# Attention passages split in PSUM, maxima four to a step with the mask added on VectorE, and a first gate in three ranges beside the mixing layer

## What is computed

```
x = x + ln(rwkv_block(ln(x)))      # time mixing (a scan), then channel mixing: squared relu, 512 wide
x = x + ln(moe_16(ln(x)))          # 16 experts of 64, grouped top-4 gate, plus a shared one of 128
x = x + ln(delta_net(ln(x)))       # 16 heads of 8, two decaying memories, q, k with rotary positions
x = x + ln(gqa_moe(ln(x)))         # h = x + gqa(rms(x)); h + moe of 8 dense experts, top 2
```

```
gate:  scores = sigmoid(x @ w_gate.T); best 2 of 4 groups; best 4 experts of these; weights normed
gqa:   attn = q k^T / sqrt(8), causal: where(j <= i, attn, -inf); softmax; @ v    # 16 heads of 8, 4 kv heads
```

## Time and profile before

| | us |
|---|---|
| median of 3 runs | 1586.7 (1578.39 to 1589.89) |
| profiled execution | 1584.72 |
| its span | 1583.5 |
| PE, DVE, ACT, POOL busy | 1204.8, 1098.2, 715.5, 697.1 |
| granted TensorE clock, mean | 0.878 |

### The profile page before, as it was taken

The page is one execution under the profiler, slowest core; times in us unless marked ns, Lnnn a source line. Parts: engine busy times, 40 slices in busy tenths (PEclk is TensorE's granted clock), DMA queues, the critical chain, the costliest instruction groups (busy, mean ns, idle before and its releaser), DMA issues.

```text
span 1583.5 us, 19095 instructions
## 1 busy us (share of the span) xinstructions
PE 1204.8 (76%) x6080; PEld 571.9 (36%) x6080; DVE 1098.2 (69%) x2477; ACT 715.5 (45%) x1576; POOL 697.1 (44%) x849
## 2 busy tenths in 40 slices
PE   3414988999998567665649687998899889989873
PEld 1212454555554223232313232444343434343222
DVE  5888546455555699898959675868686878687032
ACT  4644682255555201212130266556565556555741
POOL 7324672455455387858550122133412441244244
PEclk9756987999999698787865698999999999999995
DMA  3000013222220000020225101111010201000010
GB/s 102 0 1 7 38 51 70 74 63 66 62 73 27 11 0 1 0 55 0 45 40 79 23 1 26 35 17 33 4 32 14 37 4 32 4 1 2 2 40 14
DMA packets 33634, 46.99 MB, mean 30 GB/s; under 512 B 4991, under 2 KB 18175, under 8 KB 33215
## 3 DMA queue, kind: packets, MB, share of 16 engines
q1 hardware_dynamic: 30942, 43.84, 12.9%
q10 hardware_dynamic: 2592, 1.93, 0.4%
HBM read 39.08 MB, written 6.68 MB: 29 GB/s over the span
## 4 chain that ended last, share of the span: by engine, by line
PE 38%; DVE 29%; POOL 14%; issue 10%; ACT 8%; DMA 1%; ACTq 0%; POOLq 0%; DVEq 0%
PE PS L585 9%; DVE SS L1074 6%; PE PS L540 5%; PE PS L568 5%; DVE RB L991 3%; DVE RB L992 3%; PE PS L630 3%; PE PS L377 2%; ACT RB L1448 2%; POOL RB L1616 2%; POOL rs L1515 2%; PE PS L255 2%; DVE st L675 2%; PE PS L363 2%; DVE PS L980 2%
## 5 line engine op out<-in xcount | busy, mean ns | idle before, releaser
L1448 ACT ACTIVATE RB<-PS 128x512 f32<-128x512 f32 (+3 forms) x768 | 326.2, 497 | 288.0 <-PE PS L568 286.7
L1074 DVE TENSOR_REDUCE SS<-PS 128x1 f32<-128x512 f32 (+3 forms) x768 | 374.2, 548 | 76.4 <-PE PS L543 64.6
L540 PE MATMUL PS<-B 96*128 96x512 bf16 (+3 forms) x768 | 258.0, 355 | 52.0 <-DVE B L1117 21.3
L1682 POOL TENSOR_SCALAR_AFFINE_SELECT RB<-RB 128x512 f32<-128x512 f32 x128 | 81.2, 634 | 429.6 <-ACT RB L1448 429.5
L568 PE MATMUL PS<-B 96*128 96x512 bf16 (+3 forms) x768 | 235.5, 334 | 29.8 <-ACT RB L1448 28.7
L585 PE MATMUL PS<-RB,B 128*32 128x512 f32 (+3 forms) x1536 | 169.5, 513 | 8.2 <-ACT RB L1455 7.9
L1616 POOL TENSOR_TENSOR RB<-RB,B 128x512 f32<-128x512 f32 x64 | 83.5, 1307 | 132.2 <-DVE RB L926 99.3
L540 PEld LDWEIGHTS PS<-B 96*128 96x128 bf16 x768 | 77.1, 101 | 160.0 <-DVE SS L1074 83.6
L445 PE MATMUL PS<-RB,w_hspread 128*128 128x512 f32 x128 | 80.6, 764 | 61.9 <-POOL RB L1638 52.3
L926 DVE TENSOR_TENSOR RB<-RB,PS 128x512 f32<-128x512 f32 x72 | 49.0, 682 | 110.1 <-ACT RB L1327 80.4
L543 PE MATMUL PS<-w_msk,w_identb 128*128 128x128 bf16 x512 | 118.8, 234 | 0.0
(11 more groups left out here) (229 smaller groups left out, 2044.0 us busy)
## 6 DMA issues: line engine op xcount, KB each, us to landing
B<-scrW SPq DMA_DIRECT2D x128, 128.0 KB, 3.0
B<-scrQ SPq DMA_DIRECT2D x72, 128.0 KB
scrQ<-B SPq DMA_DIRECT2D x6, 384.0 KB, 2.6
B<-scrK SPq DMA_DIRECT2D x36, 64.0 KB
X<-in_x SPq DMA_DIRECT2D x8, 256.0 KB, 9.7
out_dram<-X SPq DMA_DIRECT2D x8, 256.0 KB, 3.0
B<-in_w SPq DMA_DIRECT2D x3, 576.0 KB, 4.6
B<-in_zeros SPq DMA_DIRECT2D x9, 128.0 KB
```

Source lines behind the costliest of these rows:

```text
L540: ins = pe.matmul(p[:, 0:w], qs[u % 3][:, h, 128 * i:128 * i + 128], keys_of(u, h)[:, 512 * c:512 * c + w], start=True, stop=not diagonal)
L1074: dve.tensor_reduce(MX[:, u % 2, i, h, c:c + 1], bank(bank_of["first", u, n])[:, 0:first_width(i, c)], AX, ALU.max).then_inc(s["mx1"], 1)
L1448: act.activation(RB[:, 4 * (step % 3) + z, 0:w], bank(bank_of["score", step, z])[:, 0:w], ACT.Exp).then_inc(s["ex2"], 1)
```

## The change

Three edits.

1. The passages. The rest (L1046) is written back into its PSUM bank; the second part is a ScalarE copy out of PSUM; the third part is subtracted on VectorE out of PSUM. R2 is gone. The banks are given back after the third part. The two memsets of slice 6 go from VectorE to GpSimd.
2. The maxima. The mask matmul is gone. `highest` takes diagonal products with `tensor_tensor_reduce`: it adds the mask (128 x 512 bf16, zeros then the triangle), writes the sum back to PSUM and the maximum to MX. Unit 1's maxima stay five to a step; from step 20 on those of units 2 to 7 go four to a step without a gap.
3. The first gate. Three ranges of 8, 8 and 16 tiles instead of two halves. Units 0, 1, 2 of the experts stand in steps 20, 21, 22 of the mixing layer, the cuts of range 0 in unit 2. Range 1 is routed in the experts' steps 3 to 8, range 2 in 11 to 17. Banks, rows and the order of SP's loads follow.

```diff
+        def maxima_at(step):
+            if step < 20:
+                return [(1, n) for n in range(5 * step, min(5 * step + 5, 96))]
+            return [(2 + m // 96, m % 96) for m in range(4 * (step - 20), 4 * (step - 20) + 4) if m < 6 * 96]
...
+        RANGES = [(0, 8), (8, 8), (16, 16)]
+        FIRST_UNIT = 20
...
             def cut_n(g):
-                pe.wait_ge(s["cut_n"], g // 4 + 1)
-                i = 4 if g >= 4 else 0
+                pe.wait_ge(s["cut_n"], range_of(g) + 1)
+                i = 1 + g if g < 2 else next_d()
...
+            def experts(v):
+                if v == 2:
+                    cut_n(0)
+                    cut_n(1)
+                if 0 <= v - 3 < 9 * NG:
+                    out_m(v - 3)
+                if 9 <= v < 11:
+                    cut_n(v - 7)
+                if 18 <= v < 22:
+                    cut_n(v - 14)
+                for g, k in head_slices(v):
+                    head_d(g, k)
+                if v < 9 * NG:
+                    gate_up_m(v)
...
+                if step >= FIRST_UNIT:
+                    experts(step - FIRST_UNIT)
+            for v in range(NG + 15 - FIRST_UNIT, MOE_STEPS):
+                experts(v)
...
-                diagonal = c == i // 4
-                ins = pe.matmul(p[:, 0:w], qs[u % 3][:, h, 128 * i:128 * i + 128],
-                                keys_of(u, h)[:, 512 * c:512 * c + w], start=True, stop=not diagonal)
-                if diagonal:
-                    ins = pe.matmul(p[:, w - 128:w], identb[:, :], msk[:, 0, :], start=False, stop=True)
-                ins.then_inc(s["mm1"], 1)
+                pe.matmul(p[:, 0:w], qs[u % 3][:, h, 128 * i:128 * i + 128],
+                          keys_of(u, h)[:, 512 * c:512 * c + w], start=True, stop=True).then_inc(s["mm1"], 1)
...
             def highest(u, n):
-                dve.tensor_reduce(MX[:, u % 2, i, h, c:c + 1], bank(bank_of["first", u, n])[:, 0:first_width(i, c)],
-                                  AX, ALU.max).then_inc(s["mx1"], 1)
+                w = first_width(i, c)
+                p = bank(bank_of["first", u, n])[:, 0:w]
+                if c == i // 4:
+                    ins = dve.tensor_tensor_reduce(p, p, msk[:, 512 - w:512], 1.0, LOWEST, ALU.add, ALU.max,
+                                                   MX[:, u % 2, i, h, c:c + 1])
+                else:
+                    ins = dve.tensor_reduce(MX[:, u % 2, i, h, c:c + 1], p, AX, ALU.max)
+                ins.then_inc(s["mx1"], 1)
...
                 if k == 6:
                     stats(b, x_tile, "e", 8)
-                    own.done(dve.memset(batch(B[4], b), 0.0))
-                    own.wait()
-                    dve.memset(VA[:, 8 * b:8 * b + 8, :, 8:9].rearrange("p i k e -> p (i k) e"), 1.0).then_inc(s["va_e"], 1)
                 if k == 9:
-                    cut_e(b, 0, cutq[b][0], R2[b][:, 0:512], 128, 8.0 ** -0.5, s["cq_e"])
+                    rest_e(b, 0, cutq[b][0], 128, 8.0 ** -0.5)
                     if b:
                         dve.wait_ge(s["sk_e"], 32 * b)
-                    cut_e(b, 1, cutk, R2[b][0:64, 512:1024], 64, 1.0, s["ck_e"])
+                    rest_e(b, 1, cutk, 64, 1.0)
+                    last_e(b, 0, cutq[b][0], 128, s["cq_e"])
+                    last_e(b, 1, cutk, 64, s["ck_e"])
                 if k == 10:
-                    cut_e(b, 2, cutq[b][1], R2[b][:, 0:512], 128, 8.0 ** -0.5, s["cq_e"])
+                    rest_e(b, 2, cutq[b][1], 128, 8.0 ** -0.5)
+                    last_e(b, 2, cutq[b][1], 128, s["cq_e"])
...
-            def cut_e(b, n, o, rest, rows_, scale, last):
+            def rest_e(b, n, o, rows_, scale):
                 p = bank(bank_of["pj_e", b, n])[0:rows_, :]
                 dve.wait_ge(s["r_e"], 4 * b + n + 1)
-                dve.scalar_tensor_tensor(rest, p, scale, o[:, 0, :], ALU.mult, ALU.subtract).then_inc(s["cut_e"], 1)
-                dve.wait_ge(s["cut_e"], 3 * b + n + 1)
-                own.done(dve.tensor_copy(o[:, 1, :], rest))
-                own.wait()
-                dve.tensor_tensor(o[:, 2, :], rest, o[:, 1, :], ALU.subtract).then_inc(last, 1)
+                dve.scalar_tensor_tensor(p, p, scale, o[:, 0, :], ALU.mult, ALU.subtract).then_inc(s["cut_e"], 1)
+            def last_e(b, n, o, rows_, last):
+                p = bank(bank_of["pj_e", b, n])[0:rows_, :]
+                dve.wait_ge(s["cm_e"], 3 * b + n + 1)
+                dve.tensor_tensor(o[:, 2, :], p, o[:, 1, :], ALU.subtract).then_inc(last, 1)
...
+                    for n, o, rows_ in ((0, cutq[b][0], 128), (1, cutk, 64)):
+                        act.wait_ge(s["cut_e"], 3 * b + n + 1)
+                        act.activation(o[:, 1, :], bank(bank_of["pj_e", b, n])[0:rows_, :], ACT.Copy).then_inc(s["cm_e"], 1)
...
+            def experts(v):
+                if v == 3:
+                    score_n(2)
...
+                if step == 17:
+                    score_n(0)
+                if step == 19:
+                    score_n(1)
...
+            weights_out(0)
+            for m in range(4):
+                for h in range(2):
+                    sp.dma_start(CW[m][64 * h:64 * h + 64, :],
+                                 scrW[2 * m + h:2 * m + h + 1, 0:512].to_broadcast([64, 512])).then_inc(s_w[m], 16)
             sp.wait_ge(s["vv_b"], 8)
             sp.dma_start(WW[:, :, :], I["wL1"]).then_inc(s["w_ww"], 16)
             sp.dma_start(cs, I["rope"]).then_inc(s["w_cs"], 16)
...
-                if m == 24:
+                if m == 12:
                     weights_out(1)
+                if m == 26:
+                    weights_out(2)
```

230 lines of the change are left out of this document (123 added, 107 removed).

## The result

| | before | after |
|---|---|---|
| median | 1585.7 us (4 runs) | 1562.7 us (4 runs, 1558.6 to 1565.1) |
| profiled execution (span) | 1584.7 (1583.5) | 1561.3 (1560.0) |
| ratio | | 0.986, 95% interval 0.981 to 0.990 |

The change gave 23 us (1.4%) where 52 were predicted. The new time lies in the predicted range (1505 to 1575), which reaches that far only because it takes in the rivals (two of them at 1557 and 1559). The likeliest case did not happen: the direction came out, the size did not. Ratios are always against the kernel before as measured beside each kernel; its medians ran from 1584.7 to 1589.3 us, so medians of different experiments compare to a few us only. All medians here are of undisturbed executions; one of the four of the kernel with plain maxima took 4702 us and is left out. Where the time went is read first from the same views as before.

What follows compares the result with a forecast made beforehand. It took VectorE to bound the scan stage and TensorE, with VectorE close behind, the last attention. 1584.7 less 34 (attention), 14 (passages) and 4 (gate) gives 1532.7, so 1533 us, range 1505 to 1575.

Steps and rivals of the forecast that it cites:

- The likeliest case: Whole kernel: all three parts gain as forecast, giving 1533 us, own range 1505 to 1553, chance 0.60.
- Where VectorE's work counts in the scan stage: Layer 1's scan with the passages: VectorE bounds the stretch, so work taken off it gains 14 us, between 5 and 16.
- The stretched L1050: Passages: subtraction falls from 2.31 to 0.69 us with its source in PSUM, five times, 8.1 us gained; casts go, 4.9.
- The memsets: Passages, slice 6: moving the memset of 1024 elements from VectorE to GpSimd gains 2.7 us and delays only the passage.
- Slice 10's bank: Passages: TensorE's slice 10 waits for the last part instead of the rest, a step later, so costed at nothing.
- The attention: Last attention: 5.6 us per unit, 39 in seven units, less 5.1 in unit 0, so 34 us gained, between -9 and 67.
- the masks: Last attention: dropping 64 mask matmuls per unit frees TensorE, 3.2 us gained per unit, between 2.6 and 3.8.
- the spreading: Last attention: four maxima in every step from step 20, instead of five in most, gains 3.3 us per unit, between 0 and 6.
- the dearer maxima: Last attention: maxima that add the mask cost VectorE 0.08 us more each, giving back 0.9 us per unit.
- the prediction's third rival: Last attention: no gain on TensorE, masks lie in time it waits anyway, spreading only moves queues; 1557 us, chance 0.13.
- the two rivals of a dearer maximum: Last attention: new maximum 0.2 us dearer gives 1559 us, chance 0.12; at half rate, 0.33 dearer, 1616 us, chance 0.10.
- The gate: First gate: only eight tiles and two cuts come before the first experts, 4 us gained, between -3 and 8.

Runs made afterwards that it cites:

- the kernel with plain maxima: Changed kernel with plain maxima in place of the maxima that add the mask, causal mask left out of the computation: 1561.0 us, ratio 0.983.
- the order put right in both kernels: Slice 10 put behind the next batch's slice 1 and the value products, in the changed kernel (1557.7 us) and in the kernel before (1579.9 us).
- the other order alone: Kernel before with only slice 10 put behind the next batch's slice 1 and the value products: 1579.9 us, ratio 0.996.
- with nothing in their place: Kernel before with the mask matmuls left out, plain maxima still five to a step: 1576.1 us, ratio 0.993.
- the division first: VectorE's division ahead of its step's maxima: kernel before 1569.4 us, with only the mask in the maximum 1561.7, with only four maxima a step 1548.8, changed kernel 1541.9.
- the masks alone: Kernel before with the mask added by VectorE in the maximum, maxima still five to a step: 1579.2 us, ratio 0.995.

## Why the prediction was right or wrong

**Where VectorE's work counts in the scan stage** was the step that failed first: 14 us predicted, minus 1.4 measured. I read "VectorE busy 195 of 224 us" as "VectorE sets the end" for the whole stretch, so that each microsecond off it came out. In most steps it does set the end: in 5.6 of 5.6 us without a passage, in 13.2 of 13.4 with slice 9, and there the work that went came out nearly whole (3.9 and 3.5 us of work, 3.6 us of time each). But 87% is an average, and more than half of the work that went stood where VectorE stands still or then began to: the memsets in the steps of slices 6 and 7, where GpSimd's rstd and the addition behind it end last; slice 10, where the held bank and TensorE's queue then ended last (no idle time before, 4.4 and 4.6 us after); and the end, where VectorE had 17.5 idle of 31.4 us. VectorE did 17.1 us less in the stage and stood idle 18.6 us longer.

**The stretched L1050** was right as a duration: 2314 ns became 685 (L1088). Of the 8.1 + 4.9 us that I booked for it and the casts, 2 x 3.6 = 7.2 came out, in the steps with slice 9. In those with slice 10 nothing did. With the order put right in both kernels these steps take 10.8 us after and 10.6 before, since the other order alone takes L1050 out of GpSimd's way there (2.73 to 0.69 us).

**The memsets** were costed with the wrong sign: plus 2.7 where the runs show minus 2.7. The prediction did name the place (GpSimd gets them before its rstd) and then said that they "delay only the passage"; the queue behind that rstd also holds the scans' add and product.

**Slice 10's bank** was dismissed in half a sentence ("it is a step later, so nothing"). TensorE's order runs ahead of VectorE's within a step, and at the end of the stage steps have no scans between them: these steps became 1.4 and 1.6 us longer although VectorE had 2.9 us less to do in each, and the tail 1.8.

**The attention** was forecast at 34 and gave 19; its terms were mis-sized. Per unit, 5.6 against 2.8 (3.3 at a clock of 1.00). Term by term: the masks 3.2, measured 1.4 to 1.9 in a light unit (2.3 with nothing in their place) and 0.4 to 1.0 in a heavy one with the division first; the spreading 3.3, measured 0.9 to 1.3 in a light unit, 2.1 to 2.3 with the division first, and then 2.6 to 3.3 in a heavy one; the dearer maxima 0.9 back, measured 0.2 to 0.45; unit 0's 5.1, measured 2.2. The two large terms were taken as if nothing stood next in line. For the spreading the next thing was in the rows that I had read: the prediction's third rival named "L1117's bank", and I gave it 0.13. That rival came nearest, 15 us in seven units less 5 in unit 0. With the masks alone TensorE's busy time fell by 2.7 us in the light unit (67.6 to 64.9), and the unit by 1.85: the rest came back as waits.

**The price of the new operation** was set too high, 0.08 against 0.03 us from start to start, and the two rivals of a dearer maximum are out. I had added the start-to-start time of a second small instruction; it runs beside the next maximum.

**The gate** came out near its forecast: predicted 4, measured 5.9, 8.4 in the kernel with this part alone, and 3.8 on average over all profiles. That it fits so well is partly luck. The prediction's own sum gives 253.7 - 250.7 = 3.0 and takes 4, and two misses in it cancel. The copies of the first cuts ended at 244.9 us where I had 250.7: the first two units' products ran ahead of the last gate product and not behind it, and the two cuts took one round trip, not two. What I costed at nothing, SyncE's loads ahead of the ninth broadcast ("not needed for some 10 us"), took 3.5 us: issued at 253.0, it was needed at 264.4 and came at 267.1, behind 1.9 MB.

**Not settled**: what holds a light unit at 68.3 us now. TensorE is busy 64.2 of them, ScalarE 44.8, VectorE 59.0; TensorE's waits that are left are many and short. Nor is it shown why mask matmuls that take 3.8 us by their distances, 3.0 by busy time, are worth 2.3 at most, nor why the heavy and the light unit divide the gain so differently.

## What to carry to other kernels

A busy share of 87% is an average of steps in which the engine never waits and of steps in which it stands still. Read the share step by step, and ask at which of them the work that goes away stands, before a microsecond off the engine is booked as a microsecond won. When a buffer is to be held longer, or a small operation is moved to another engine, read what stands behind it in that queue, and on the producer's queue, step by step. And before thinning out the work in front of a wait, look which operation frees the buffer that is waited for: moving one division ahead of two maxima, an edit of three lines, was worth 21 us, nearly as much as the whole change.

## What the hardware showed beyond that

A maximum with a mask added from SBUF runs at a plain maximum's rate: 708 ns against 685 for 512 columns, and in unit 0's maxima its 141-ns accumulator read starts together with VectorE's next operation (both at 838.67 us), so that neither waits for the other. A subtraction of two SBUF tiles of 512 columns took 2.73 us beside GpSimd's operations of 1024 elements and 0.69 behind them, a cast 0.97 and 0.43, so that a mere change of order was worth 2.6 us a step. TensorE's granted clock was 0.50 (1.2 GHz) through unit 0's maxima in every kernel, 58 to 65 us at a stretch, although TensorE was busy 39.6 of the 46.2 us there; when it came up again varied by several us from kernel to kernel. Later drops inside a unit (TensorE was busy 73.2 of 82.0 us in the one shown above) cost 1.1 to 1.6 us each, as much as the terms that these experiments were to tell apart: units had to be compared by their granted clock first.
